# A projection and causal-attention kernel whose causal stage becomes one written-out sequence, with its loads, stores and value products in another order

## What is computed

```python
x = L0_attn_x                                   # (4, 1024, 256)
xn = _layernorm(x, axis=-1)
# first layer: causal attention, queries are xn itself
kv = xn @ W.T;  K, V = kv[..., :d], kv[..., d:]
scores = jnp.einsum('bqd,bkd->bqk', xn, K) + mask      # mask: -inf above the diagonal
ya = xn + jnp.einsum('bqk,bkd->bqd', jax.nn.softmax(scores, axis=-1), V)
# second layer, its projections
q = xn @ Wq;  k = xn @ Wk_c @ Wk;  v = xn @ Wv_c @ Wv  # 16 heads of 16
q, k = _apply_rope(q, sin, cos), _apply_rope(k, sin, cos)
# ... 16-head attention, output projection, norm, shared and routed experts, norm
```

## Time and profile before

| | |
|---|---|
| median of 3 runs | 1648.71 us (1640.29 to 1651.46) |
| profiled execution | 1648.22 us, of which the span is 1646.5 us |
| projections, from PE's first transpose to its last product | 11.0 to 166.1 us |
| causal stage, from its first score to its last value product | 173.3 to 336.2 us |
| third block, first product of PE | 344.2 us |
| PE busy over the span | 88% |
| DVE busy over the span | 72% |

### The profile page before, as it was taken

The page is one execution under the profiler, slowest core; times in us unless marked ns, Lnnn a source line. Parts: engine busy times, 40 slices in busy tenths (PEclk is TensorE's granted clock), DMA queues, the critical chain, the costliest instruction groups (busy, mean ns, idle before and its releaser), DMA issues. The chain is left out here.

```text
span 1646.5 us, 21956 instructions
## 1 busy us (share of the span) xinstructions
PE 1452.0 (88%) x7856; PEld 838.3 (51%) x7856; DVE 1182.6 (72%) x1706; ACT 833.9 (51%) x1503; POOL 361.5 (22%) x316
## 2 busy tenths in 40 slices
PE   7988787957999999999999999869999999999994
PEld 4555565722333333333333333237888878878873
DVE  3676544568888888888888888446776876876542
ACT  2444333303888888888888888833214133042130
POOL 1222830135140000000000000013143252352441
PEclk9999999966999999999999999979999999999997
DMA  5779565352343323333333331021230321311211
GB/s 191 238 261 335 195 217 151 75 93 65 70 109 58 54 45 54 51 59 59 59 58 59 59 59 53 34 81 40 86 83 22 104 52 52 104 24 55 53 14 13
DMA packets 105826, 145.83 MB, mean 89 GB/s; under 512 B 24048, under 2 KB 74624, under 8 KB 105728
## 3 DMA queue, kind: packets, MB, share of 16 engines
q1 hardware_dynamic: 83840, 102.93, 25.2%
q0 software_dynamic: 10784, 23.76, 6.8%
q10 hardware_dynamic: 11104, 17.83, 3.4%
HBM read 80.90 MB, written 63.06 MB: 87 GB/s over the span
## 5 line engine op out<-in xcount | busy, mean ns | idle before, releaser
L1480 DVE TENSOR_REDUCE i_saT<-h_sq 128x2 f32<-128x1024 f32 x512 | 601.2, 1219 | 78.4 <-PE h_sq L1364 78.3
L1446 ACT ACTIVATE h_p<-h_sk 128x512 f32<-128x512 f32 x999 | 543.5, 596 | 180.5 <-PE h_sk L1385 159.1
L1385 PE MATMUL h_sk<-h_q,h_k 50*128 50x512 f32 x999 | 251.0, 495 | 57.4 <-ACT h_p L1446 55.9
L1398 PE MATMUL h_po<-h_p,h_v 128*32 128x512 f32 x2048 | 275.4, 610 | 2.0 <-ACT h_o L1453 1.6
L1385 PEld LDWEIGHTS h_sk<-h_q,h_k 50*128 50x128 f32 x999 | 94.7, 184 | 339.6 <-ACT h_p L1446 326.9
L1364 PE MATMUL h_sq<-h_k,h_q 48*128 48x512 f32 x1024 | 196.3, 450 | 25.8 <-DVE i_saT L1480 14.2
L1703 PE MATMUL f_ob<-w_experts,f_h 128*128 x768 | 179.5, 393 | 0.0
L1703 PEld LDWEIGHTS f_ob<-w_experts,f_h 128*128 128x128 f32 x768 | 143.8, 188 | 31.6
L1364 PEld LDWEIGHTS h_sq<-h_k,h_q 48*128 48x128 f32 x1024 | 100.9, 194 | 97.9 <-DVE i_saT L1480 77.2
L1616 POOL TENSOR_TENSOR f_h<-h_place,f_h 128x512 fp32r<-128x512 f32 x64 | 83.6, 1311 | 289.0 <-ACT f_h L1768 289.0
L1764 ACT ACTIVATE f_x1p<-f_pair 128x1024 fp32r<-128x1024 f32 x8 | 8.2, 1026 | 226.1 <-PE f_pair L1016 226.1
(11 more groups left out here) (213 smaller groups left out, 1741.4 us busy)
## 6 DMA issues: line engine op xcount, KB each, us to landing
h_q<-q_d SPq DMA_DIRECT2D x84, 128.0 KB, 5.9
h_k<-k_d SPq DMA_DIRECT2D x84, 128.0 KB, 6.9
ot_d<-h_o ACTq DMA_DIRECT2D x32, 256.0 KB, 4.2
q_d<-t_parts SPq DMA_DIRECT2D x12, 512.0 KB, 5.0
k_d<-t_parts SPq DMA_DIRECT2D x12, 512.0 KB, 5.2
h_place<-xs_d SPq DMA_DIRECT2D x8, 530.0 KB, 4.3
p_xin<-in_L_attn_x SPq DMA_DIRECT2D x8, 512.0 KB, 5.3
xn_d<-p_xn SPq DMA_DIRECT2D x8, 512.0 KB, 3.8
```

The source lines that it names most:

```text
L1385: ins = nc.tensor.matmul(spread_banks[bank_at(f + g)], k6[r][at, p, j * P:(j + 1) * P], q6[r][at, p, c * CH:(c + 1) * CH], start=True, sto ...
L1398: ins = nc.tensor.matmul(po[h * VW:(h + 1) * VW, :], vh[n % RING][:, j, h, :], probs[u % PR][:, h, :], start=j == 0, stop=j == QT - 1)
L1446: nc.scalar.activation(probs[u % PR][:, h, :], spread_banks[bank_at(f)], ACT.Exp, scale=DH ** -0.5).then_inc(exp_done, 1)
L1480: nc.vector.tensor_reduce(halfmax[n % 2][:, m, :], sq[slot % 2][:, :, :], AX.X, ALU.max)\
```

## The change

In the projections the engines' slots are reordered and shifted. DVE does `norm` of chunk c+1 first in its slot, and `variance` one chunk further ahead (c+2) behind the rotation; ACT's `root` goes to the end of its slot and to c+2 likewise. The exchange of neighbours, POOL's sine products and `turned` each go in two halves with their own signals. SP issues the store of xn ahead of the stores of the causal inputs. What the stage waited for at its end (stores of values and rotated parts, the exchange of the last chunk, one rounding on ACT) is waited for, or done, in the next block; the two blocks share their semaphores, so none are cleared between them, and the identity and mask are made once, in the first block.

In the causal stage the hardware loop is gone: 32 tiles are one sequence on each engine. The value products of tile u-1 come after the turns of tile u and the scores of tile u+2. SP issues all loads, in two halves (queries and keys; values and x), and ACT issues the stores. The values of the next sequence are split in two pieces at tiles 4 and 5 of the sequence before; those of sequence 0 in two pieces at tile 0. At the seam only the queries and keys of sequence 0 are loaded ahead of the block, not its values and x.

In the third block PE's wait for the identity moves behind the first products.

```diff
     def slot(it, s, c):
+        if exists(c, 1):
+            norm(*near(it, s, 1))
         if exists(c, -2):
             low(*near(it, s, -2))
         if exists(c, -1):
             turn(*near(it, s, -1), near(it, s, -2) if exists(c, -2) else None)
-        if exists(c, 1):
-            variance(*near(it, s, 1))
-        if exists(c, 1):
-            norm(*near(it, s, 1))
+        if exists(c, 2):
+            variance(*near(it, s, 2))
         if exists(c, -1):
             turned(*near(it, s, -1))
...
+    def partners(self, s):
+        for half in range(2):
+            at = slice(half * KD, (half + 1) * KD)
+            self.nc.vector.stream_shuffle(self.swap[:, at, :], self.qk[:, at, :],
+                                          [i ^ 1 for i in range(32)]).then_inc(self.sw_done[s], 1)
...
                 sp.wait_ge(causal_in, CausalInputs.LOADS * 16)
-                for name, each in st.items():
+                for name in ("xn", "xnT", "kaT", "va"):
                     for s in range(2):
...
+                inputs.load_rows(sp, 0, rows_in[0])
+                inputs.load_keys(sp, 1, keys_in[1])
+                inputs.load_rows(sp, 1, rows_in[1])
+                for b in range(2, B):
+                    for u in ((b - 1) * QT - 2, (b - 1) * QT - 1):
+                        wait.ge(scored[u % 2], u // 2 + 1)
+                    inputs.load_keys(sp, b, keys_in[b % 2])
+                    for u in ((b - 1) * QT - 2, (b - 1) * QT - 1):
+                        wait.ge(ya_done[u % 2], u // 2 + 1)
+                    inputs.load_rows(sp, b, rows_in[b % 2])
...
+                score(0)
+                score(1)
+                for u in range(U):
+                    turn(u)
+                    if u + 2 < U:
+                        score(u + 2)
+                    if u:
+                        mix(u - 1)
+                mix(U - 1)
...
+                turning.high(act, NCH // 2 - 1, 0)
+                for u in range(U):
...
+                    if u == 0:
+                        for n in range(PIECES):
+                            round_values(0, n)
+                    if u >= 2:
+                        store(u - 2)
+                    if b + 1 < B and SPLIT_AT <= u % QT < SPLIT_AT + PIECES:
+                        round_values(b + 1, u % QT - SPLIT_AT)
...
-                pe.wait_ge(const_set, 2)
                 for m in range(ITEMS):
                     item(0, m)
                 for m in range(HELD):
                     item(1, m)
+                pe.wait_ge(const_set, 2)
                 turn_maxima(0)
```

More of the change, by code:

```diff
@@ L493, in _ @@
                 norm(0, 0)
+                variance(0, 1)
                 slots(dve, slot)
@@ L675, in _ @@
                 wait = Waits(sp, passed)
-                inputs.load(sp, 1, 1, loaded[1])
-                with sp.Fori(0, B // 2) as it:
-                    for u in range(U):
-                        s, i = where(u)
-                        wait.ge(ya_done[u % 2], it * (U // 2) + u // 2 + 1)
-                        sp.dma_start(ya_d[bass.ds((it * 2 + s) * S + i * P, P), :], ya[u % 2][:, :])\
-                            .then_inc(ya_stored[u % 2], 16)
+                inputs.load_rows(sp, 0, rows_in[0])
@@ new lines, in score @@
+                def score(u):
+                    b, i = where(u)
+                    if u % QT == 0 and b:
+                        pe.wait_ge(keys_in[b % 2], (b + 1) // 2 * CausalInputs.LOADS * 16)
+                    if u >= 2:
+                        pe.wait_ge(exp_done[u % 2], u // 2)
+                    n = (i + 1) * P
+                    for c in range(0, n, CH):
+                        w = min(CH, n - c)
+                        for k in range(KD):
+                            ins = nc.tensor.matmul(sc[u % 2][:, c:c + w], qT[b % 2][:, k, i * P:(i + 1) * P],
+                                                   kT[b % 2][:, k, c:c + w], start=k == 0, stop=k == KD - 1)
+                    ins.then_inc(scored[u % 2], 1)
@@ L808 @@
+                finish(U - 1)
 class FeedForwardWeights:
```

373 lines of the change are left out of this document (192 added, 181 removed).

## The result

The changed kernel takes 1607.57 us (median of 4 runs, 1603.50 to 1610.51), against 1650.09 of the kernel before on the same chip (4 runs, 1640.29 to 1651.86). The ratio is 0.9742, with a 95% interval of 0.9711 to 0.9773: 2.6% faster. I had forecast 1605, in a range of 1594 to 1622.

What follows compares the result with a forecast made beforehand. No engine was full; PE's time through the first two stages, and the waits stretching it, bound the kernel. -18.8 - 5.0 - 17.1 - 4.0 = -44.9 from 1648.2 gives 1603.3; plus 1.7, forecast 1605, range 1594 to 1622.

Steps and rivals of the forecast that it cites:

- Norm first: Projections: with the norm at the slot's head PE sets the pace, 16.36 us a slot; projections -18.8 us.
- rival 3: Projections: the norm is still late through another wait of DVE's slot, slots stay near 20.5 us: 1624 us, chance 7%.
- What the cover costs: Projections: the same bytes in shorter slots fit, 311 GB/s at a DMA share of 0.92; costed at nothing.
- Rival 2: Projections: transfers set the pace, 2 us a slot, so 12 us go back: 1617 us, chance 12%.
- The sum beside the sines: Projections: each half of the sum could wait for one sine product of 1.27 us, already within the slot's 17 us.
- Seam: Between projections and causal stage: most waits moved or gone, the next block begins sooner; -5.0 us (3 to 6).
- The causal stage's start: Two low parts wait for POOL's long instructions, the second ending 18.0 us into the block, or 22.5 if asked later.
- Rival 1: Causal stage's start: no hold, products of tile 0 start near 163: 1600 us, 1596 with a warm seam, chance 12%.
- Steady part: Causal stage after its start: same instructions, waits taken away one by one, 1.6 us left; whole stage -17.1 us.
- rival 4: Causal stage: stores issued by ACT slow every tile, 74 us more at 3.80 us an issue: 1679 us, chance 3%.
- Third block: PE's first products start some 0.4 us into the block instead of 4.43; -4.0 us (0 to 4.4).
- After it: Whole kernel: 1.7 us added for waits of a few tenths that a sum on paper misses.

Runs made afterwards that it cites:

- e5: Kernel before, with the third block's wait for the identity moved behind PE's first score products: 1647.60 us against 1651.03, ratio 0.9988.
- e3: Changed kernel with DVE's norm behind turn and exchange again, variance still two chunks ahead: 1615.82 us, ratio 0.9807.
- e7: Changed kernel with the old order of variance, root and norm; exchange and sum stay in halves: 1616.44 us, ratio 0.9799.
- e12: Changed kernel with the old order of variance, root and norm, and exchange and sum in one piece each: 1622.57 us, ratio 0.9839.
- e11: Changed kernel with the exchange and the rotation's sum in one piece each, norm still first: 1608.45 us, ratio 0.9737.
- e1: Changed kernel, but POOL's third long instruction waits for both low parts of sequence 0: 1604.25 us, ratio 0.9729.
- e2: Changed kernel with one low part for sequence 0 instead of two: 1604.86 us, ratio 0.9733.
- e4: Changed kernel with value products of tile u in their own turn, behind the scores of tile u+2: 1618.13 us, ratio 0.9817.
- e6: Changed kernel with ACT issuing loads of sequences 2 and 3, SP the stores, and roundings at tiles 6 and 7: 1614.20 us, ratio 0.9800.
- e8: Changed kernel with the next values rounded at tiles 6 and 7, not 4 and 5: 1608.35 us, ratio 0.9747.
- e10: e9, with POOL issuing its first twelve loads for the heads only when the inputs of sequence 3 have landed: 1597.97 us, ratio 0.9681.
- e9: Changed kernel with POOL's third long instruction behind the low parts and roundings at tiles 6 and 7: 1602.65 us, ratio 0.9718.

## Why the prediction was right, step by step

Place by place, predicted and measured in the profiled runs: projections -18.8, -19.4; seam -5.0, -5.0; causal stage -17.1, -14.4; third block -4.0, -4.1; after that +1.7 as friction, +3.8. Sum: -44.9 + 1.7 = -43.2 against -39.1. That single places agree to a few tenths is in part luck: the kernel before and e5, the same code up to there, differ by 2.7 us in the length of the causal stage (162.9 and 165.5).

- **Norm first.** The slot of 16.36 us came as worked out, and rival 3 is out with it. The extra 0.6 is the first chunk, which reached its second transposes 0.6 earlier; that lies within the scatter of 29.14 to 30.93 between runs and is no gain. The reading of the cause was too simple: I laid all of the 2.1 us wait and its sequel on the alternation of the earlier trace rows. e3, e7 and e12 split the 17.0 us in three: 5 x 1.5 = 7.5 for the norm behind the exchange, 5 x 0.9 = 4.4 for the whole pieces, 3 x 1.7 = 5.1 for a low clock. The waits stand beside that clock but are no certain cause of it, since e12 has the same waits without it. The changed order takes all three away at once, so the sum came out. For that the norm at the slot's head is enough: e11 has whole pieces and the same 16.36 us.
- **What the cover costs.** Nothing, as taken: a share of 0.92, as estimated, and 322 GB/s for 311. Rival 2 is dead.
- **The sum beside the sines.** By the rule of the Trainium skill ("SBUF — State Buffer", "Who interferes with whom") the halves could each wait for a sine product; the trace agrees for the first half, 2.27 instead of 1.23, and it was hidden as reckoned. One remark of the prediction is wrong: the old order did not keep the low part of the values apart from POOL's products (the earlier trace rows shows the two together). Only the sum was new there.
- **Seam.** Right in total. What each of the steps moved away from the seam gives was not tested, but for the halves: without them it would be 1.4 us less (e11), and the prediction had no term for them there. ACT's take to the block's start is 1.2 us (taken: 0.8), and PE starts with it (taken: 0.3 later).
- **The causal stage's start, the step that was mis-sized.** The mechanism was right, low parts that wait for POOL's 4.5 us. But I chose the earlier of two phases: products 18.1 us into the block, where it was 22.2. The values landed for ACT at 11.2 us into the block, and DVE asked 1.2 us after POOL's third long instruction had begun; I had taken 10.5. That is +4.1, and the other value that I gave (22.5) would have been right. The phase hung on 1.2 us, which no row of before could give, but it is no accident of one run: in all eight kernels that have the new stage without e1's or e2's edit the first value products start 22.2 us behind the first score. From there to the end it took 126.3 us and not 128. That is not because of fewer waits: they are 2.1 us, where I left 1.6, but PE's products took 124.2 where I had 126.4. So one error gave back part of the other. Rival 1, no hold, is out. e1 and e2 show the mechanism directly.
- **Steady part.** Stores on ACT cost nothing that shows (rival 4 is dead): 0.33 to 0.39 us an issue while the stage runs. e4 values the later products at 10.5 us of the stage, e6 the loads' place at 5.9 (with roundings at tiles 6 and 7). What it gives that scores cross the old end of the loop was not tested by itself. What I named as a danger, a late load of values at tiles 4 and 5, did not strike here but did in e1, as soon as the stage started earlier.
- **Third block.** 4.39 us of start gained at its place, in the changed kernel and in e5.
- **After it.** 3.8 us of lead are given back, where I had 1.7. From PE's first product of the third block to the first `f_ob` product, fourteen kernels (the same there but for the wait for the identity, which the change and e5 move) take 794.7 to 800.1 us (before 795.8, changed 799.3, e5 796.3, e8 799.2, e11 800.1, e12 794.7), without regard to what was edited ahead: this looks like the scatter of single runs and not like a reply to the change. Part of the changed run's is one place in the fourth block, first in the changed kernel, then in the kernel before:

```profile
1072.58 7.67 PE L1747 MATMUL f_pair<-f_x1p,w_routed 128*128 128x512 f32 x23 [7.37 <-DVE h_place L1123]
```

```profile
1112.56 5.67 PE L1695 MATMUL f_pair<-f_x1p,w_routed 128*128 128x512 f32 x17 [5.29 <-DVE h_place L1071]
```

What makes it wait 2.1 us longer stays open.

## What to carry to other kernels

Before an instruction is split in two, look at what runs on the engine that excludes it: each piece can wait for one whole instruction there, so let one side wait (e1) or ask once (e2); to cut the long ones was not tried. When a stall is taken away, look up which transfers now start earlier and what they meet: here 8.5 us won at a stage's start became 2.7 at its end, until the loads for the next stage were moved out of the way as well (e10, which also has the later roundings). And read the granted clock beside a wait before it is priced: with the same 2.2 us wait, slots of one and the same kernel took 18.7 and 20.5 us.

## What the runs showed of the hardware that I had not expected

- Two DVE instructions of 1.2 us beside POOL's row took 9.83 us (changed), one of twice the size 5.32 (e2), and two with POOL held back 2.36 (e1). In these runs the two engines take turns: the second low part did not get in before POOL's next instruction (changed), nor did any of the four norm instructions of a slot before one of POOL's products (e3).
- Twelve DMAs of 128 KB, issued by POOL, raised the landing of a 1 MB load on another queue from 6.5 to 17.4 us and the median landing of a 128 KB store from 2.8 to 6.9 (one stretch, e10 and e9). It is not that their packets were small: in the rows of e9 they are 2.7 KB in the mean and those of the load 1 KB, and they took 8 times as much of the DMA engines' time. The Trainium skill says of this on "DMA: Bandwidth & Descriptors", section "Queues, rings and completion order", that each DMA engine goes round the queues that have work, a packet at a time. That a second queue with work slows the first agrees with e9; no run here shows the turns themselves.
- PE's granted clock differed between runs of the same code: 1.00 and 0.94 from 66 to 84 us (before and e5, in both a wait of 2.1 to 2.2 us in each slot), 0.98 and 0.93 from 263 us on. The slot that starts at 66.02 in the kernel before takes 18.74 us, that at 64.15 in e5 20.42, so the clock is worth 1.7 us there. Within the kernel before it went from 1.00 (66 to 84 us) to 0.92 (84 to 105 us) with the same waits. What made it fall stays open.
